# The place of the edge-group matmuls in TensorE's order: end of their own slot, or middle of the next one

## The reference

```python
xn  = layernorm(x)                                   # 6250 x 256
agg = segment_sum(xn[src], dst, 6250)                # 100,000 gathered rows, added by target
deg = segment_sum(ones, dst, 6250)
x   = x + xn @ W_self + agg / max(deg, 1) @ W_neigh + b
xn  = layernorm(x) * gamma + beta
w, e = softmax over the top 2 of xn @ Wr + br        # 8 experts, 2 for each node
y   = sum over the two: w * (gelu(xn @ W1[e] + b1[e]) @ W2[e] + b2[e])    # 256 -> 512 -> 256
out = x + y
```

## Time and profile before

| | |
|---|---|
| median of 3 runs | 1264.21 us (1263.98 to 1268.24) |
| the profiled execution, its own time | 1265.15 us |
| its span, first to last instruction | 1263.1 us |
| TensorE matmuls busy | 1095.5 us, 87% of the span |
| GpSimd (POOL) busy | 942.5 us, 75% |
| VectorE busy | 865.6 us, 69% |
| mean granted TensorE clock | 0.969 of full speed |

### The profile page before, as it was taken

How to read it: one execution, slowest core, us unless ns; L and a number is a source line. 1 busy time by engine, 2 the same in 40 slices (tenths; PEclk the granted TensorE clock), 3 DMA queues, 4 the chain that set the end, 5 groups by cost and what they waited for, 6 DMA issues and landing times.

```text
span 1263.1 us, 22169 instructions
## 1 busy us (share of the span) xinstructions
PE 1095.5 (87%) x6356; PEld 971.6 (77%) x6357; DVE 865.6 (69%) x2812; ACT 435.7 (34%) x812; POOL 942.5 (75%) x980
## 2 busy tenths in 40 slices
PE   0479999989987999999899898987989887988987
PEld 0368888979976888998788787776778776877977
DVE  7886766777676767768767675855667764655447
ACT  7723322323433334434434443433224312211131
POOL 7677777777667777777777777777777777777774
PEclk9999999999998999999999898998999999999989
DMA  9999987866556476666756665656687668766766
GB/s 351 328 317 377 301 294 262 287 199 211 179 166 202 146 253 198 221 199 207 213 183 199 187 191 185 195 162 209 188 259 221 211 213 275 227 219 210 230 206 227
DMA packets 163993, 287.57 MB, mean 228 GB/s; under 512 B 25632, under 2 KB 93344, under 8 KB 163744
## 3 DMA queue, kind: packets, MB, share of 16 engines
q1 hardware_dynamic: 115280, 153.36, 36.5%
q0 software_dynamic: 45696, 124.88, 32.6%
q10 hardware_dynamic: 2896, 7.87, 1.7%
HBM read 228.81 MB, written 57.20 MB: 226 GB/s over the span
## 4 chain that ended last, share of the span: by engine, by line
PE 54%; POOL 13%; DVE 12%; issue 9%; DMA 7%; SPq 2%; ACT 1%; DVEq 0%; POOLq 0%; ACTq 0%
PE bank L966 17%; PE bank L1042 13%; POOL ring L689 11%; PE bank L1068 8%; PE bank L1076 5%; PE bank L995 3%; PE bank L954 3%; PE bank L997 2%; DMA ring<-feature_table,src_sb 2%; DMA heap<-in_x 1%; PE bank L1092 1%; DVE heap L1480 1%; POOL pair L711 1%; DVE agg L1323 1%; PE bank L1103 1%
## 5 line engine op out<-in xcount | busy, mean ns | idle before, releaser
L689 POOL DMA_INDIRECT ring<-feature_table,src_sb x756 | 743.1, 983 | 248.1 <-issue 218.9
L966 PE MATMUL bank<-ring,onehot 128*128 128x257 f32 x1544 | 393.3, 399 | 100.0 <-issue 57.9
L966 PEld LDWEIGHTS bank<-ring,onehot 128*128 128x128 f32 x1544 | 302.0, 199 | 157.9 <-issue 109.9
L868 ACT ACTIVATE heap<-heap 128x512 f32<-128x512 f32 x139 | 87.8, 632 | 335.2 <-DVE heap L1480 335.2
L1480 DVE TENSOR_TENSOR heap<-bank,b_sb 128x512 f32<-128x512 f32 x139 | 95.9, 690 | 145.0 <-PE bank L1042 77.4
L1068 PE MATMUL bank<-heap 128*128 x728 | 182.5, 395 | 13.7 <-DVE y_out L1489 7.9
L1042 PE MATMUL bank<-row_t,heap 128*128 128x128 f32 x1456 | 179.1, 277 | 0.7 <-DVE heap L1480 0.6
L1042 PEld LDWEIGHTS bank<-row_t,heap 128*128 128x128 f32 x1456 | 173.4, 194 | 2.6 <-issue 1.1
L1068 PEld LDWEIGHTS bank<-heap 128*128 128x128 f32 x728 | 137.2, 196 | 31.8 <-issue 14.7
L1323 DVE SCALAR_TENSOR_TENSOR agg<-bank,in_first,agg 128x257 f32 x196 | 94.4, 482 | 96.5 <-PE bank L966 62.9
L1281 DVE TENSOR_TENSOR onehot<-iota,target 128x512 f32<-128x512 f32 x196 | 134.2, 685 | 7.1 <-DVE xf L1340 4.8
(11 more groups left out here) (193 smaller groups left out, 1250.6 us busy)
## 6 DMA issues: line engine op xcount, KB each, us to landing
heap<-in_w SPq DMA_DIRECT2D x139, 512.0 KB, 5.0
expert_out<-empty_row SPq DMA_DIRECT2D x68, 256.0 KB
ring<-feature_table,src_sb POOLq DMA_INDIRECT x756
row<-expert_rows SPq DMA_DIRECT2D x91, 128.5 KB, 4.3
xf<-in_x SPq DMA_DIRECT2D x49, 128.0 KB
ff<-feature_table SPq DMA_DIRECT2D x49, 128.0 KB
expert_out<-inside SPq DMA_DIRECT2D x46, 128.0 KB
expert_out<-y_out SPq DMA_DIRECT2D x45, 128.0 KB
```

The lines of the kernel that those rows point to most:

```text
L689: pool.indirect_dma_start(group_row(t, i)[:, 0:D], None, x if t < RAW else table, bass.IndirectOffsetOnAxis(src_sb[:, k:k + 1], 0)).then_i ...
L868: act.activation(hid[s], hid[s], ACT.Gelu).then_inc(S.gelu, 1)
L966: last = pe.matmul(bank[t % 2][:, 0:D + 1], onehot[:, q, i, :], group_row(t, i), start=(i == 0), stop=(i == GT - 1))
```

## The change

`group(t - 1)` is called in slot t behind the front part, and `group(t)` is no longer called at the slot's end. No instruction is added or removed, and the orders of VectorE, ScalarE, POOL and SP are the same as before.

```diff
                 for j in tiles_in(t, "hidden"):
                     hidden_of_rows(main, j)
+                if 1 <= t <= NG:
+                    group(t - 1)
                 for n in blocks_in(t, "count"):
...
                     results(main, j)
-                if t < NG:
-                    group(t)
                 if t == CLAIMS:
```

## The result

The changed kernel took **1351.8 us** (median of 4 runs, 1348.5 to 1354.5), the kernel before 1266.2 beside it: a ratio of 1.0664 with a 95% interval of 1.0635 to 1.0692. That is slower by about 85 us; 57 were forecast, and the range ended at 1347. The profiled execution took 1348.5, with a span of 1346.4.

What follows compares the result with a forecast made beforehand. TensorE and POOL were taken to push each other, TensorE behind, until 372 us, then POOL's own work plus a tail. Sum: 1265.15 + 4 + 38.4 - 1.2 + 0.4 + 14 + 1 = 1321.8, so 1321 us; range 1288 to 1347.

Steps and rivals of the forecast that it cites:

- Which engine, which wait, which direction: TensorE's first layers wait for VectorE's bias behind the add, and POOL then waits for TensorE: slower, chance 0.90.
- First stretch, +38.4 in 26 places: Slots 13 to 60, ending with group 59: first layers wait for the bias at 26 places, +38.4 us, bounds about 22 and 45.
- the price of 2.60: From a group's end through add, one-hot and bias on VectorE to the next first layer: 2.60 us, less TensorE's work meanwhile.
- the three kinds of places: Back part without second layer: 6, 17.2 us; second layer but longer chain: 11, 14.1; ended by second layer two units earlier: 9, 7.2.
- The gathers of group 14, -1.2: In the first stretch, an earlier TensorE wait of 1.21 us for group 14's gathers goes away: -1.2 us.
- The clock, 0: Half clock after TensorE's new long waits was taken as 0 us, by a row at full speed after 2.45 us.
- The rival that I gave 0.16: TensorE's clock falls at the new waits in both stretches: +20 us, 1341 us in all; chance 0.16.
- After 372 us, +14: From group 67 to slot 93, 16 places cost 16.8 us; less POOL's lead of 3.55 and other terms, +14, bounds 0 and 18.
- The start, +4: Group 8 behind block 1's transposes, which wait for DMA, delays SP's loads and TensorE's first unit: +4 us, bounds 0 and 6.7.
- The tail, +1: At the kernel's end, the last block's transposes need the last group's add: +1 us, between nothing and 2.60.
- that only the first stretch costs: Rival: POOL's lead takes the whole second stretch, so the 14 us there go: 1307 us; chance 0.12.
- The faster rival: Front parts fill waits for gathers, TensorE runs ahead and POOL's waits for it go: 1253 us; chance 0.05.

Runs made afterwards that it cites:

- the run with filled waits: Changed kernel plus 233 matmuls of 128 columns, results unused, ahead of layers that wait in slots 13 to 95: 1329.3 us, 22.5 less than the changed kernel.
- the run with groups 60 to 96: Kernel before, with the new place only for groups 60 to 96, all others at the end of their own slot: 1285.0 us, ratio 1.0160.
- the last experiment: Kernel before, with the group ahead of the second layer or product in seven slots (19, 24, 29, 34, 43, 45, 59): 1254.7 us, ratio 0.9910.

## Why the prediction was right, and where it was wrong

- **Which engine, which wait, which direction**: right. First layers wait for the bias, the bias stands behind the add, and the delay reaches POOL. The experiments that moved the group ahead of the first layers, shortened the chain or cut it show it from three sides.
- **First stretch, +38.4 in 26 places**: right. 25 waits of 35.4 us, and 0.16 of lost overlap at each, which the price of 2.60 held: 39.4. They stand in 25 of the 26 forecast slots (22 has none), and the three kinds of places come to 17.0, 15.2 and 7.3 us against 17.2, 14.1 and 7.2. With the overlap, slot 17 has 3.22 against 3.06 (119.43, below) and slot 48 has 3.39 against 2.84. Most of that difference is the 0.43 us before the one-hot at 335.33, where the order shown above has the load of four block numbers into VectorE's registers (line 186), which I had not priced, though the kernel before has it in the same place. The one large miss of the first kind is slot 37, with 1.25 against 2.69: there the transposes ahead of the first layer wait 1.23 us for the same add and take over a part.
- **The gathers of group 14, -1.2**: right, that wait is gone.
- **The clock, 0**: this is the step that failed. I set one wait in the same stretch that left the clock full (187.53 in the earlier trace rows) against one that did not, and took nothing. It was 21.7 us by the rows of slots 13 to 94, and the run with filled waits got 22.5 back, a little of it at the start. The runs show that many waits together do bring half clock, although a single one need not. The rival that I gave 0.16 had the size right, +20. That rival and the forecast are not alternatives: with all its other terms the sum would have been 1341.
- **After 372 us, +14**: too small. Alone that stretch cost 20 (14 to 26). Its first layers waited 16.1 + 14 x 0.16 = 18.3 against the 16.8 forecast, half clock added 5.4 in slots 61 to 94, and POOL's lead took 89.4 - 85.1 = 4.3, near the 3.55 forecast. With 18.3 and 5.4 put in, the sum of the prediction gives 20.9. One reading was loose: seven of POOL's 20 waits in the earlier trace rows end behind 372.50, but they take 0.30 each, its usual step.
- **The start, +4**: the direction right, the size near its upper bound: +7 (3 to 11). The load of the biases moved from 74.55 to 80.89, 6.3 later.

```profile
80.89 0.33 SPq L571 DMA_DIRECT2D b_sb<-in_b  x1
```

- **The tail, +1**: nothing that can be measured, -1 (-5 to +2).
- **The rivals**: that only the first stretch costs is refuted by the run with groups 60 to 96. The faster rival's idea, front parts that fill waits, did not come about here, since the new waits are far larger; but a group that fills a wait does make the kernel faster, by 10 us, and POOL's waits fall by 12.5 with it, as the last experiment shows.

Worked out at the measured sizes: 7 + 36.3 + 4 (overlap) + 16.3 in the first part, 20 in the second, 0 behind it: 83.6, against 56.6 forecast in the same terms and 83.4 between the two profiled executions (1348.5 - 1265.15). Of the 27 that were missing, up to 21.7 are half clock. The 7 and the 20 are known to 4 and 6 us only, so that the agreement to 0.2 is luck.

## What to carry to other kernels

In a loop over two engines that each take their instructions in order, moving a step later moves everything that stands behind its answer on the other engine. Its price is the chain from the step to the next need, less the work that still stands between, place by place; that arithmetic held to a few per cent in sum here, though not at each place. Where a change turns 7 waits of over 1 us into 19, count the lost clock as part of the forecast and not as a rival. And look for the place where independent work fills a wait: behind the instruction that the other engine must answer, ahead of the one that needs the answer.

## What the runs showed of the hardware that was not expected

A wait does not decide by itself whether half clock follows. In the changed kernel a first layer ran at full speed after 3.06 us, another at half speed after 3.63, and a second layer took 3.10 us instead of 1.89 after only 2.01:

```profile
119.43 2.02 PE L1042 MATMUL bank<-dst_i,heap 128*128 128x128 f32 x16 [3.06 <-DVE heap L1480]
...
187.32 3.76 PE L1042 MATMUL bank<-dst_i,heap 128*128 128x128 f32 x16 [3.63 <-DVE heap L1480]
...
304.70 3.10 PE L1076 MATMUL bank<-heap 128*128 128x256 f32 x8 [2.01 <-DVE agg L1515]
```

So one row could not settle the term, whichever it was. What tells the three apart stays open. Measured is the sum over many waits: 16.3 us of half clock for 36.3 us more of idle time in the first stretch.
